# Layer 2's expert tiles: W1 copied by GpSimd to a fixed buffer and used as the stationary operand, without transposes of the result

## What is computed

```
h = silu(z @ W1[e])        # 512
y = h @ W2[e]              # 128
```

## Time and profile before

| | us |
|---|---|
| median of 3 runs | 3185.36 |
| lowest, highest | 3180.08, 3189.39 |
| the profiled execution's own time | 3190.76 |
| its span, first to last instruction | 3189.0 |

### The profile page before, as it was taken

The page is one execution under the profiler, slowest core; times in us unless marked ns, Lnnn a source line. Parts: engine busy times, 40 slices in busy tenths (PEclk is TensorE's granted clock), DMA queues, the critical chain, the costliest instruction groups (busy, mean ns, idle before and its releaser), DMA issues. The chain is left out here.

```text
span 3189.0 us, 63316 instructions
## 1 busy us (share of the span) xinstructions
PE 2487.6 (78%) x20966; PEld 1889.2 (59%) x20966; DVE 2069.1 (65%) x6419; ACT 1395.7 (44%) x2573; POOL 1154.8 (36%) x1149
## 2 busy tenths in 40 slices
PE   3588778858779999999778888169996688887766
PEld 0254444447767787877656666147774365666755
DVE  6477648868667766677559788333333577784578
ACT  1466610013256666656456555022221465563432
POOL 2355512321054555455401344700000556634711
PEclk9988889969889999999989888579998788898988
DMA  4200001132100000000020010111111111100001
GB/s 142 98 31 27 20 27 40 39 113 70 34 1 1 1 1 1 0 1 1 16 71 12 28 36 23 46 47 54 53 54 53 43 33 32 39 10 10 1 25 33
DMA packets 126020, 108.78 MB, mean 34 GB/s; under 512 B 15548, under 2 KB 105942, under 8 KB 124888
## 3 DMA queue, kind: packets, MB, share of 16 engines
q1 hardware_dynamic: 106840, 80.58, 8.3%
q0 software_dynamic: 8192, 16.79, 1.8%
q10 hardware_dynamic: 10752, 8.39, 0.8%
HBM read 70.59 MB, written 35.13 MB: 33 GB/s over the span
## 5 line engine op out<-in xcount | busy, mean ns | idle before, releaser
L1318 POOL TENSOR_TENSOR l1ffn_hid<-l1ffn_act 128x512 f32<-128x512 f32 x256 | 330.5, 1294 | 341.7 <-ACT l1ffn_act L1459 308.0
L1600 DVE SCALAR_TENSOR_TENSOR l1ffn_acc<-bank,l1ffn_w,l1ffn_acc 128x128 f32<-128x128 f32 x960 | 269.3, 343 | 150.0 <-PE bank L1403 142.7
L1403 PEld LDWEIGHTS bank<-l_w_ahead,l1ffn_hid 128*128 128x128 f32 x2048 | 265.2, 191 | 68.7 <-issue 49.9
L1403 PE MATMUL bank<-l_w_ahead,l1ffn_hid 128*128 128x128 f32 x2048 | 271.7, 276 | 37.9 <-DVE l1ffn_acc L1600 37.5
L1456 ACT ACTIVATE l1ffn_act<-scores,l1ffn_b 128x512 f32<-128x512 f32 x256 | 176.3, 689 | 203.6 <-PE scores L214 203.4
L2231 ACT ACTIVATE l_probs_t<-bank 128x512 f32<-128x512 f32 x256 | 140.4, 596 | 105.9 <-PE bank L229 104.8
L2299 DVE TENSOR_REDUCE l_top<-scores 128x16 f32<-128x1024 f32 x128 | 155.2, 1213 | 43.1 <-PE scores L2130 42.6
L212 PE MATMUL scores<-l1ffn_z_high,l1ffn_w_high 128*128 128x512 f32 x384 | 173.5, 452 | 0.0
L2302 DVE TENSOR_TENSOR l_probs<-scores,l_top 128x1024 f32<-128x1024 f32 x128 | 156.8, 1225 | 13.7 <-DVE l_top L2299 0.5
L229 PEld LDWEIGHTS bank<-ident,l_probs 128*128 128x128 f32 x1024 | 130.0, 155 | 49.2 <-issue 25.5
L923 DVE SCALAR_TENSOR_TENSOR l0moe_acc<-scores,l0moe_w_now,l0moe_acc 128x128 f32<-128x128 f32 x512 | 137.7, 344 | 32.6 <-PE scores L871 32.6
(11 more groups left out here) (440 smaller groups left out, 6284.5 us busy)
## 6 DMA issues: line engine op xcount, KB each, us to landing
l2ffn_xs<-scratch_l_in SPq DMA_DIRECT2D x136, 64.0 KB, 1.8
scratch_l_out<-l2ffn_y SPq DMA_DIRECT2D x34, 256.0 KB, 2.3
x_all<-scratch_x SPq DMA_DIRECT2D x32, 256.0 KB, 3.4
l_ctx_t<-in_ctx_t SPq DMA_DIRECT2D x32, 256.0 KB
l_w_ahead<-in_l_w SPq DMA_DIRECT2D x3, 2048.0 KB, 12.7
x_all<-in_x SPq DMA_DIRECT2D x16, 256.0 KB, 3.0
l0mix_ctx<-in_ctx SPq DMA_DIRECT2D x16, 256.0 KB, 3.3
scratch_x<-l0mix_x_out ACTq DMA_DIRECT2D x16, 256.0 KB, 2.3
```

The costliest lines, as they stand in the source:

```text
L1318: pool.tensor_tensor(hid[:, e % K], act1[:, e % K], act3[:, e % K], ALU.mult)\
L1403: mm = pe.matmul(bank[5 + k][:, t * D:(t + 1) * D], hid[:, e % K, t * P:(t + 1) * P], w2[:, e, :], start=True, stop=True)
L1600: mm = v.scalar_tensor_tensor(out=acc[:, t, :], in0=y, scalar=w[:, h, t, e:e + 1], in1=before, op0=ALU.mult, op1=ALU.add)
```

## The change

GpSimd gets a loop over the tiles: it reads the tile's expert into a register and copies the 128 x 512 block of W1 into one of four fixed buffers `w_now`. TensorE's `hidden(j)` now takes four 128-column parts of that buffer as the stationary operand, one after the other, and the 128 columns of `x_t` as the moving one, so that the result lies in the bank already transposed. `hid`, `turn_hidden` and `hid_out` with their semaphores are gone; silu writes `hid_t` directly. The hidden banks are three (1 to 3) in place of two. `hidden(j)` waits for `w_copied` beside its other waits; GpSimd's copy of tile j waits for `made_h` of tile j - 4; `silu(j)` waits until `output(j - 2)` is made, and `output(j)` for `silu(j)`.

```
-    RING = 8
+    RING, WR, HB = 8, 4, 3
+        w_now = ph.sb("w_now", [P, WR, L2_H])
...
             def _(pool):
                 pool.memset(zeros[:, :], 0.0).then_inc(filled, 1)
+                pool.wait_ge(listed, 2)
+                ahead.wait(pool)
+                for j in range(NT):
+                    e = pool.value_load(tile_of_e[0:1, j:j + 1], min_val=0, max_val=E - 1)
+                    reuse(pool, made_h, j - WR + 1)
+                    pool.tensor_copy(w_now[:, j % WR], w1[:, bass.ds(e, 1), :].rearrange("p a f -> p (a f)"))\
+                        .then_inc(w_copied, 1)
...
                     pe.wait_ge(turned_out, j // 4 + 1)
-                    reuse(pe, hid_done, j - 1)
+                    pe.wait_ge(w_copied, j + 1)
+                    reuse(pe, hid_done, j - HB + 1)
                     t = j % 4
-                    pe.matmul(bank[1 + j % 2][:, :], x_t[:, j // 4 % 2, t * P:(t + 1) * P],
-                              w1[:, bass.ds(chosen[j], 1), :].rearrange("p a f -> p (a f)"), start=True, stop=True)\
-                        .then_inc(made_h, 1)
-
-                def turn_hidden(j):
-                    pe.wait_ge(hid_done, j + 1)
-                    reuse(pe, hid_t_done, j - 1)
-                    transposes(pe, bank[3 + j % 2], [hid[:, j % 2, c * P:(c + 1) * P] for c in range(C)], ident)\
-                        .then_inc(hid_turned, 1)
+                    for c in range(C):
+                        mm = pe.matmul(bank[1 + j % HB][:, c * P:(c + 1) * P], w_now[:, j % WR, c * P:(c + 1) * P],
+                                       x_t[:, j // 4 % 2, t * P:(t + 1) * P], start=True, stop=True)
+                    mm.then_inc(made_h, 1)
 
                 def output(j):
                     q, t = j // 4, j % 4
-                    pe.wait_ge(hid_t_done, j + 1)
+                    pe.wait_ge(hid_done, j + 1)
...
                 hidden(1)
-                turn_hidden(0)
                 for j in range(NT):
...
                     if j + 2 < NT:
                         hidden(j + 2)
-                    if j + 1 < NT:
-                        turn_hidden(j + 1)
                     output(j)
...
                     act.wait_ge(made_h, j + 1)
-                    reuse(act, hid_turned, j - 1)
-                    act.activation(hid[:, j % 2], bank[1 + j % 2][:, :], ACT.Silu).then_inc(hid_done, 1)
+                    reuse(act, made_y, j - 1)
+                    act.activation(hid_t[:, j % 2], bank[1 + j % HB][:, :], ACT.Silu).then_inc(hid_done, 1)
...
-                hid_out(0)
                 output_slots()
-                for j in range(NT):
-                    if j + 1 < NT:
-                        hid_out(j + 1)
-                    if j % 4 == 3:
-                        y_out(j // 4)
+                for q in range(QUADS):
+                    y_out(q)
```

More of the change, by code:

```diff
@@ L2495, in l2_ffn @@
         inside, jump, moved = ph.sb("inside", [P, K * TILES, E]), ph.sb("jump", [P, E]), ph.sb("moved", [P, K, TILES])
-        xs, hid, hid_t, y = ph.sb("xs", [P, RING, D]), ph.sb("hid", [P, 2, L2_H]), ph.sb("hid_t", [P, 2, L2_H]), ph.sb("y", [P, 2, N])
+        xs, hid_t, y = ph.sb("xs", [P, RING, D]), ph.sb("hid_t", [P, 2, L2_H]), ph.sb("y", [P, 2, N])
+        w_now = ph.sb("w_now", [P, WR, L2_H])
         w_in, filled, padded = ph.sem("w_in"), ph.sem("filled"), ph.sem("padded")
@@ L2501, in l2_ffn @@
         stored = [ph.sem("stored0"), ph.sem("stored1")]
-        turned, turned_out, made_h, hid_done = ph.sem("turned"), ph.sem("turned_out"), ph.sem("made_h"), ph.sem("hid")
-        hid_turned, hid_t_done, made_y, y_done = ph.sem("hid_turned"), ph.sem("hid_t"), ph.sem("made_y"), ph.sem("y")
+        turned, turned_out, w_copied, made_h = ph.sem("turned"), ph.sem("turned_out"), ph.sem("w_copied"), ph.sem("made_h")
+        hid_done, made_y, y_done = ph.sem("hid"), ph.sem("made_y"), ph.sem("y")
         rows_out = picks.rows_out.rearrange("(q t p) d -> q p t d", t=4, p=P)
@@ L2670, in _ @@
                 tile_list()
[L2672 to L2675, removed]
                 def y_out(q):
```

## The result

The changed kernel takes 3106.64 us (median of 6 runs, 3086.95 to 3112.67) against 3188.1 us before (median of 6, 3180.08 to 3194.08). The ratio is 0.9735, with a 95% interval of 0.9706 to 0.9764. That is 81.5 us less; 83 were forecast. The profiled execution of the changed kernel has a span of 3110.9 us.

What follows compares the result with a forecast made beforehand. TensorE's in-order work bounds layer 2's expert stage: 345.7 us falls to 260.7, 85 less; 2 given back for joints leaves 83. From 3190.76 that gives about 3108, and the median, 5.4 lower, 3102; range 3092 to 3130.

Steps and rivals of the forecast that it cites:

- Silu's stall: Once per group TensorE waits for silu queued behind x_t on ScalarE; 34 stalls of 0.8 go, 27 us.
- Head: Start of the stage: second output waits while VectorE does slot arithmetic between two copies; this stall, 1.6 to 2 us, goes.
- GpSimd, 1.0 us a copy, covered: GpSimd's tile loop: copy 1.0 us, pace with register read about 1.0 to 1.3, hidden below TensorE's 1.79 a tile.
- TensorE's queue, 1.6 us a turn: TensorE's sequencer: one turn about 1.6 us (bounds 1.5 and 1.9), hidden under the 1.79 that TensorE needs.
- VectorE's steps at the head: VectorE's two-input steps beside GpSimd's first copies may wait for them; between 0 and 1 us, taken as 0.
- The joints: Allowance for joints between TensorE's records that no row shows; 2 us given back from the 85 saved.
- The clock term: Half-speed clock at the stage's start, from 2097.4 to about 2102; costs 2.3 us (bounds 1.3 and 4).
- GpSimd's pace: Rival: GpSimd's register read doesn't overlap its copy, 2.18 us a tile; 44 us saved, 3141; chance 0.11.
- the slower case: Rival: at TensorE's wait for w_copied, the copy holds it longer than the transposes; 16 us more, 3201; chance 0.04.
- the queue's: Rival: TensorE's sequencer sets the pace, 1.9 us a tile; 70 to 85 saved, or 63, about 3120; chance 0.07.
- narrow matmuls that don't pipeline: Rival: hidden's 128-column records step 275 ns, hidden takes 2.2 us; 93 us more, 3278; chance 0.01.
- No gain: Rival: loads or something else outside TensorE holds 10 us a group; 3185; chance 0.03.

Runs made afterwards that it cites:

- silu_slots: silu_first with VectorE's slot arithmetic put ahead of the first copy of the transposed result; 3160.29 us, ratio 0.992 to the kernel before.
- wide_unturned: Changed kernel with the old 512-column hidden matmul, no GpSimd copy or wait, result not transposed (output not the reference's); 3101.94 us, ratio 0.9722 to before.
- silu_first: Kernel before with two lines swapped on ScalarE: silu of the next tile ahead of x_out of the next group; 3163.26 us, ratio 0.992.
- copy_four: Changed kernel with four GpSimd copies of the W1 block a tile, each waiting for the one before; 3228.13 us, ratio 1.0138 to the kernel before.
- read_twice: Changed kernel with one more, unused register read of tile_of_e per tile on TensorE's queue; 3130.34 us, ratio 0.9824 to the kernel before.
- copy_twice: Changed kernel with two GpSimd copies of the W1 block a tile, the second waiting for the first; 3111.73 us, ratio 0.9755 to the kernel before.
- both_f32r: hidden_f32r with hid_t also fp32r and W2 rounded once by GpSimd, so the output matmul is fp32r too; 3090.03 us, ratio 0.9715 to before.
- hidden_f32r: Changed kernel with x_t and w_now declared fp32r, so the hidden matmul runs at lower precision; 3065.87 us, ratio 0.9627 to the kernel before.

## Why the prediction was right, step by step

- *The bound*: TensorE, before and after. Right; it is at 220.0 of 220 us.
- *Transposes, 58.5 us*: 59.8 between silu_slots and wide_unturned.
- *Silu's stall, 27 us*: 27.4 by the groups of silu_first (33 stalls of 0.83; the prediction counted 34 of 0.8). It needed the matmul row and the timeline together: the waits alone call 15.4 us of it.
- *Narrow matmuls, 5 us*: 4.9 by the groups, all costs of the new way of feeding TensorE included. The step of 0.112 from layer 3's rows held for hidden.
- *Head*: the stall was forecast as 1.6 to 2 us; it was 1.6 of waiting in the kernel before and 2.3 in silu_first. With the second spell of low clock and the shorter first one the head gave 4.1 in all. The sum leaves it 85 - 58.5 - 27 + 5 = 4.5.
- *GpSimd, 1.0 us a copy, covered*: right that it is covered, mis-sized in the term: the copy takes 0.61, nearer to the row of the memset (0.52) than to the middle between it and a two-input op. The register read does overlap it. copy_four shows that: its read for the next tile starts at 2201.3, inside the four copies of 2199.25 to 2201.89.

```profile
L2546 POOLq TENSOR_LOAD <-l2ffn_tile_of_e x1: 288/288/288, 2201.3 to 2201.3; - x1
```

- *TensorE's queue, 1.6 us a turn*: 1.4, from 2235.5 to 2236.9 in the row below, the shortest step of its group; read_twice shows that it binds at one read more.

```profile
L2565 PEldq TENSOR_LOAD <-l2ffn_tile_of_e x2: 298/300/303, 2235.5 to 2236.9; - x2
```

- *VectorE's steps at the head, 0 to 1 us*: beside GpSimd's first copies two of them grew, from 0.30 to 0.70 us and from 0.23 to 0.57; the first load is issued 11.2 us after the first step of the tile list in both kernels, so nothing was lost.

```profile
2095.23 1.28 POOL L2548 COPY l2ffn_w_now<-l_w_ahead 128x512 f32 x2 [0.18 <-issue]
2095.30 0.70 DVE L2645 TENSOR_TENSOR l2ffn_before<-l2ffn_numbers,l2ffn_before 128x136 f32<-128x136 f32 x1
2096.03 0.57 DVE L2646 TENSOR_SCALAR l2ffn_before<-l2ffn_before 128x136 f32<-128x136 f32 x1
```

This agrees with "SBUF — State Buffer" of the Trainium skill (Who interferes with whom) for the first, which has two SBUF inputs; the second has one, and its mode isn't in the trace.
- *The joints, 2 us*: there are none. The sum without them, 85, meets the stretch's 86.4.
- *The clock term, 2.3 us*: mis-sized. Hidden began at 2106.5. A mean of 0.61 over 2100 to 2112 is 9.4 us at 0.50, so the low clock ended near 2109.4, and 2.9 us at half speed cost about 1.5. In copy_twice the same start had 6 us of it, about 3. The prediction's bounds of 1.3 and 4 hold both.
- *The whole time*: 3102 forecast, 3106.64 measured. That the two lie so near is in part luck: the stretch gained 3.4 us more than the 83, and in the profiled executions a stage ahead of it took 10.3 us more than before.

The rivals: GpSimd's pace and the slower case need more than one copy's work (copy_twice, copy_four); the queue's was near but not reached (read_twice); narrow matmuls that don't pipeline are refuted by the changed kernel's rows and wide_unturned. With them goes the estimate of 2.1 us for hidden that the prediction drew from the steps of some 81 and 131 ns in "TensorE: Matmul & The Clock Gate" of the Trainium skill (Back-to-back issue gap): hidden takes 0.89 us here. *No gain* needed loads that hold 10 us a group; a group takes 7.59.

## What to carry to other kernels

When the saturated engine also does layout work, look whether another operand order gives the layout for nothing; a dynamic block that must be stationary can be copied ahead by an idle engine, if that engine's share per tile stays well below the saturated engine's. Before that, look for small in-order stalls: a swap of two lines gave 27 of the 86 us. Compare kernels by the step of their steady part as well as by a whole stretch: here a spell of low clock at the head moved two stretches by 1.5 us against each other. After such a change measure the distance to the next bound by doubling its work (copies, register reads) and don't assume it.

## What the hardware showed that I had not expected

**The clock did not rise for fp32r at 128 columns.** In both_f32r TensorE's records leave no idle from the first matmul on, and the granted clock stays 0.50 (1.2 GHz) through the whole stage; its records step 0.21 us where hidden_f32r's, at full clock, step 0.12. With one of the two products in plain fp32 the clock is 1.00. It isn't one odd execution: the mean clock of the whole kernel is 0.851 to 0.855 in all four of both_f32r, and 0.886 to 0.894 in the three fast ones of hidden_f32r. What in the mix decides was not tried.

**Stages that the change doesn't touch move by up to 20 us.** Layer 3's attention took 442 us in the profiled execution of the kernel before, 441 in that of the changed kernel and 423 in that of copy_twice, with the same code. Two of the view's stretches, first of the changed kernel, then of copy_twice:

```profile
2520.00:2570.00 50.00, 41.87 (x602) 30.77 (x599) 39.21 (x93) 30.18 (x46) 28.63 (x31) 0.86 0.13 34
...
2570.00:2620.00 50.00, 42.23 (x609) 30.69 (x609) 39.09 (x99) 29.51 (x44) 28.96 (x32) 0.86 0.12 34
```

```profile
2520.00:2570.00 50.00, 42.13 (x685) 31.41 (x684) 41.77 (x103) 33.63 (x51) 31.68 (x33) 0.97 0.13 36
...
2620.00:2670.00 50.00, 42.12 (x692) 32.28 (x690) 40.09 (x95) 30.97 (x47) 33.56 (x35) 0.94 0.15 42
```

The granted clock is 0.86 in one and 0.94 to 0.97 in the other, and more records fit into 50 us. Another stage, ahead of layer 1's experts, took 201.8 to 216.5 us in the ten profiles, 203.9 before and 214.2 in the changed kernel; from 750 to 800 us, inside it, the granted clock is 0.93 in the one and 0.81 in the other. These 10.3 us more than make up the 8.3 by which the spans differ less than the stretches. Such steps are as large as the spread of the runs (3087 to 3113 for the changed kernel), of which only one has a profile, and they are why the table above argues from the stretch and not from the whole. That a stage ends at another moment may decide which pattern the next one falls into; the runs show both patterns, but no run was made to tell what chooses.
